# Two-layer attention and expert kernel on one Trainium2 core: stage loads moved, first preload in three portions, expert results scattered per token

## The reference

```python
x = L0_attn_X                                  # (2, 2048, 256): 4096 tokens of width 256
h = _layernorm(x) * (1 + ca) + sa              # sa, ca, ga, ... from _silu(L0_c) @ L0_wmod
x = x + ga * _L0_attn_ref(h, W_q, W_k, W_v, W_o)      # 16 heads of 16, RoPE, causal
h = _layernorm(x) * (1 + cb) + sb
x = x + gb * _L0_ffn_ref(h, gate_w, expert_w)         # 8 experts, one per token (argmax)
h = _layernorm(x) * (1 + ca) + sa              # the second layer's modulation from here
x = x + ga * _L1_attn_ref(h, ...)                     # gated mix along blocks of the sequence
h = _layernorm(x) * (1 + cb) + sb
x = x + gb * _L1_ffn_ref(h, ...)                      # RMS norm, softmax over the best 2 of 8
                                                      # experts, each silu(x W1a + b) * (x W1b + b) W2 + b2
```

## Time and profile before

| what | value |
|---|---|
| runs shown | 2666.26, 2665.64, 2662.68 us; median 2665.64 |
| profiled execution, its own time | 2663.03 us |
| its span | 2661.1 us, 39725 instructions |
| granted TensorE clock, mean | 0.916 of full speed |
| busy: PE, PE weight load | 2231.8 us (84%), 1413.0 us (53%) |
| busy: DVE, ACT, POOL | 1693.0 (64%), 1260.2 (47%), 859.6 (32%) |
| HBM read, written | 150.88 MB, 85.07 MB |
| stage ends (approximate) | modulation 47, projections 244, attention 1206, output projection 1268, first experts 1506, layer1 1827, routed experts 2559, combine 2661 |

### The profile page before, as it was taken

One profiled execution on the slowest core, in us unless ns is written; L12 is line 12 of the kernel. 1 busy time (PEld: TensorE's weight loads), 2 busy tenths in 40 slices (PEclk: granted clock), 3 DMA queues, 4 the chain that ended last, 5 costly groups with the idle time before them and its releaser, 6 DMA issues. The chain is left out here.

```text
span 2661.1 us, 39725 instructions
## 1 busy us (share of the span) xinstructions
PE 2231.8 (84%) x12968; PEld 1413.0 (53%) x12968; DVE 1693.0 (64%) x2599; ACT 1260.2 (47%) x2419; POOL 859.6 (32%) x1041
## 2 busy tenths in 40 slices
PE   3984898999989899996799699853999999999930
PEld 1762233333333333325577456553888888888830
DVE  4873877777777778844688768753545555545544
ACT  1331376766757677773223344412445555545520
POOL 2445302122121211110655413543223333323256
PEclk8996699999999999998899899966999999999975
DMA  4368604042140400002860100115444344434324
GB/s 164 107 144 166 91 2 65 5 62 35 33 65 3 64 3 3 2 1 67 351 256 0 31 1 17 40 44 182 136 152 141 133 149 141 146 121 133 123 76 126
DMA packets 138336, 238.26 MB, mean 90 GB/s; under 512 B 14768, under 2 KB 101552, under 8 KB 136752
## 3 DMA queue, kind: packets, MB, share of 16 engines
q1 hardware_dynamic: 122128, 181.44, 19.8%
q0 software_dynamic: 14928, 50.35, 10.7%
q10 hardware_dynamic: 1104, 4.20, 1.1%
HBM read 150.88 MB, written 85.07 MB: 89 GB/s over the span
## 5 line engine op out<-in xcount | busy, mean ns | idle before, releaser
L892 DVE TENSOR_REDUCE tile_max<-p_m 128x2 f32<-128x1024 f32 (+3 forms) x640 | 651.9, 1061 | 172.5 <-PE p_m L751 102.8
L854 ACT ACTIVATE probs<-p_s 128x512 f32<-128x512 f32 (+3 forms) x1280 | 596.3, 534 | 273.2 <-PE p_s L764 267.7
L2052 PE MATMUL p_up<-f_xT,f_w 128*128 128x512 f32 (+1 forms) x2304 | 468.9, 352 | 8.6 <-POOL f_w L2182 8.6
L2052 PEld LDWEIGHTS p_up<-f_xT,f_w 128*128 128x128 f32 x2304 | 372.2, 189 | 62.0 <-issue 8.9
L2182 POOL TENSOR_TENSOR f_w<-f_raw,f_w 128x1024 fp32r<-128x1024 f32 x96 | 230.9, 2409 | 504.0 <-ACT f_w L2104 504.0
L751 PE MATMUL p_m<-ka,qa 96*128 96x512 bf16 (+3 forms) x1280 | 363.3, 366 | 27.1 <-PEq L327 15.3
L705 POOL TENSOR_SCALAR_AFFINE_SELECT probs<-probs 128x128 f32<-128x128 f32 x512 | 143.3, 292 | 732.2 <-ACT probs L854 724.7
L764 PE MATMUL p_s<-qa,ka 99*128 99x512 bf16 (+3 forms) x1280 | 353.5, 353 | 11.5 <-ACT probs L854 6.9
L778 PE MATMUL p_o<-probs,va 128*32 128x512 f32 (+3 forms) x2560 | 305.9, 550 | 29.5 <-POOL probs L705 29.5
L2067 PE MATMUL p_y<-f_w,f_hidden 128*128 128x256 f32 x1872 | 261.8, 286 | 23.0 <-DVE f_y L2158 11.7
L2067 PEld LDWEIGHTS p_y<-f_w,f_hidden 128*128 128x128 f32 x1872 | 241.1, 188 | 45.4 <-issue 23.5
(11 more groups left out here) (242 smaller groups left out, 2602.3 us busy)
## 6 DMA issues: line engine op xcount, KB each, us to landing
y_slots<-zeros SPq DMA_DIRECT2D x73, 512.0 KB, 5.6
f_raw<-in_W1a SPq DMA_DIRECT2D x24, 1024.0 KB, 6.5
f_raw<-in_W1b SPq DMA_DIRECT2D x24, 1024.0 KB, 8.6
f_raw<-in_W SPq DMA_DIRECT2D x24, 1024.0 KB, 11.1
qk_scr<-parts SPq DMA_DIRECT2D x48, 256.0 KB, 2.3
qa<-qk_scr POOLq DMA_DIRECT2D x42, 256.0 KB, 15.6
ka<-qk_scr POOLq DMA_DIRECT2D x42, 256.0 KB, 17.4
v_scr<-wqkv_raw SPq DMA_DIRECT2D x32, 256.0 KB, 3.1
```

Of the source, the lines that this page charges most:

```text
L854: nc.scalar.activation(probs[:, (buf * UNITS + n) % NPROBS, h, lo:CH], p_s[:, s_bank(("exp", HG * n + h), buf), lo:CH], ACT.Exp, scale=DH ...
L892: nc.vector.tensor_reduce(out=tile_max[:, 2 * hp:2 * hp + 2, i, bank], in_=p_m[:, at_bank, :, 0:width], op=ALU.max, axis=AX.X).then_inc(ma ...
L2052: last = nc.tensor.matmul(p_up[:, f % 2, ab, 0:size], w1[:, wh, ab * KT + kt, f * P:(f + 1) * P], xT[:, t % 2, xh, kt, 0:size], start=(kt, ...
```

## The change

Eight edits; line numbers of the changed kernel are some ten to forty higher.

1. Projections: ACT's loop is written out, and the first stage's load is cut in three portions of 4, 4 and 5 DMAs, issued at the end of ACT's chunks 4, 5 and 6.
2. The ones rows of the first `ka` buffer are set by POOL in the projections, between its rstd and its subtracts of the weights; those of the other two after unit 11 of attention stage 0. At the start of stages 1 to 7 PE waits for them.
3. Attention: POOL issues the load of stage s + 2 after the masks of unit 11 (the last of the second chunk) of stage s, for s = 1 to 5, in place of stage s + 3 after stage s. Buffer and order of the loads are the same.
4. `top1_experts`: the zero fill and its memset are gone.
5. `layer1`: the rows of x are 258 wide; the two new columns are the token's number plus 1 and its first choice plus 1. DVE copies the numbers out of the route table before it centers, and waits for that table; each `choose` gets one more small operation, and `owner_ids` one.
6. `routed_experts`: DVE works out each row's place among the tokens (`find_rows`, five small operations, each waiting for the one before) behind `rest_of_x`, into three buffers `y_to`. POOL scatters a tile's result with them (4 or 2 indirect DMAs, L2216 of the changed kernel) into `y_rows`, where the first choices lie in token order and then the second ones; empty rows go to a dump row. SP's stores of y are gone; its load of x waits for `find_rows` of the tile before; `take_y` and, from t = 3 on, `find_rows` wait for scatters of earlier tiles.
7. `combine`: 16 plain loads of 512 KB by SP in place of the 64 gathers, ACT does the first weighting, DVE the rest, with all 8 chunks in SBUF at once.
8. Several semaphores are kept across stages and no longer cleared between them.

```diff
 def load_first_stage(third):          # ACT, projections
+    if third == 0:
         for qk in range(2):
             act.wait_ge(parts_stored[qk], 16 * SPLIT * CPS)
         act.wait_ge(va_stored, 16 * NHG * CPS)
-    load_scores_rows(act, k, 0, k.qa0, k.ka0, k.stage0_loaded)
-    load_values(act, k, 0, k.va0[:, :, :], k.stage0_loaded)
+    load_scores_rows(act, k, 0, k.qa0, k.ka0, k.stage0_loaded, range(2 * third, 2 * third + 2))
+    if third == 2:
+        load_values(act, k, 0, k.va0[:, :, :], k.stage0_loaded)
 def chunk(i, par):
-    if isinstance(i, int) and i == NCH - 2:
-        load_first_stage()
...
     split(i, 1)
+    if isinstance(i, int) and CPS <= i < CPS + 3:
+        load_first_stage(i - CPS)
...
 root(nc, pool, k, 0)                  # POOL, projections
+pool.wait_ge(k.rstd_ready, 1)
+nc.gpsimd.memset(k.ka0[QROWS:QROWS + SPLIT, :, :], 1.0).then_inc(ones0_set, 1)
+pool.wait_ge(ones0_set, 1)
...
 for s in range(1, NBUF):              # POOL, attention
     load(s)
-for rows in ka:
-    last = nc.gpsimd.memset(rows[QROWS:QROWS + SPLIT, :, :], 1.0)
-last.then_inc(ones_set, 1)
 for s in range(NS):
     for n in diag_no:
         mask(s, n)
-    if s + NBUF < NS:
-        load(s + NBUF)
+        if diag_no[n] == 2 * TPC - 1:
+            if s == 0:
+                pool.wait_ge(diag_masked, 2 * TPC)
+                for n1 in range(1, NBUF):
+                    nc.gpsimd.memset(ka[n1][QROWS:QROWS + SPLIT, :, :], 1.0).then_inc(ones_set, 1)
+                pool.wait_ge(ones_set, NBUF - 1)
+            elif s + NBUF - 1 < NS:
+                load(s + NBUF - 1)
...
-    with sp.Fori(0, NSLOT // ST) as t:          # SP, top1_experts
-        sp.dma_start(k.y_slots[at(t, ST, ST), :].rearrange("(p u) d -> p (u d)", p=P), zeros[:, :]
-                     ).then_inc(slots_zeroed, 16)
...
+dve.wait_ge(route_loaded, 16 * ROUTE_LOADS)     # DVE, layer1, ahead of center_h
+c_own.add(nc.vector.tensor_copy(row_ids[:, :, 0], token_no))
...
 if t:                                 # SP, routed_experts, load(t)
     sp.wait_ge(turned, t)
+    sp.wait_ge(y_to_ready, t)
...
+def find_rows(t):                     # DVE, routed_experts
+    blocks = SIZES[t] // P
+    dve.wait_ge(x_loaded, 16 * t + 16)
...
+    dve.wait_ge(second_ready, 4 * t + 4)
+    if t >= 3:
+        dve.wait_ge(y_stored, 16 * blocks_to[t - 2])
+    nc.vector.tensor_copy(y_to[:, t % 3, 0:blocks], second[:, 0:blocks]).then_inc(y_to_ready, 1)
...
     if t:                             # take_y(t)
-        dve.wait_ge(y_stored, 16 * t)
+        dve.wait_ge(y_stored, 16 * blocks_to[t])
...
 if f == TURN_AT and not last_tile(t):
     rest_of_x(t + 1)
+    find_rows(t + 1)
...
+def scatter(t):                       # POOL, after the four pieces of tile t + 1
+    pool.wait_ge(y_to_ready, t + 1)
+    pool.wait_ge(y_ready, t + 1)
+    for u in range(SIZES[t] // P):
+        pool.indirect_dma_start(out=k.y_rows[:, :],
+                                out_offset=bass.IndirectOffsetOnAxis(ap=y_to[:, t % 3, u:u + 1], axis=0),
+                                in_=y[:, u, :], in_offset=None).then_inc(y_stored, 16)
...
+for i in range(NCH):                  # SP, combine; all loads ahead of the stores
+    for q in range(2):
+        row = q * SECOND + 1 + i * CH
+        sp.dma_start(ys[:, q, rows_of(i), :], k.y_rows[row:row + CH, :].rearrange("(u p) d -> p u d", p=P)
+                     ).then_inc(loaded[i], 16)
...
+nc.scalar.activation(res[:, t, :], ys[:, 0, t, :], ACT.Copy, scale=k.weights[:, 0, t:t + 1])   # x32, ACT
+nc.vector.scalar_tensor_tensor(out=res[:, t, :], in0=ys[:, 1, t, :], scalar=k.weights[:, 1, t:t + 1],
+                               in1=res[:, t, :], op0=ALU.mult, op1=ALU.add)                  # x32, DVE
```

More of the change, by code:

```diff
@@ L135, in modulation @@
         product, copied, own = m.sem("mod_product"), m.sem("mod_copied"), m.sem("mod_own")
-        x_loaded = [m.sem(f"x_loaded{b}") for b in range(B)]
+        x_loaded = k.x_loaded
         LOADS = 6
@@ L270, in normalize, with load_scores_rows @@
     nc.vector.tensor_tensor(h, h, shift, ALU.add).then_inc(done, 1)
-def load_scores_rows(engine, k, s, qa, ka, loaded):
-    for g, (qp, kp) in enumerate(zip(Q_PARTS, K_PARTS)):
+def load_scores_rows(engine, k, s, qa, ka, loaded, groups=range(len(Q_PARTS))):
+    for g in groups:
+        qp, kp = Q_PARTS[g], K_PARTS[g]
         for dst, qk, part in ((qa, 0, qp), (ka, 1, kp)):
@@ L557, in attention @@
         p_o = m.ps("p_o", [P, CH])
-        stage_loaded = [m.sem(f"stage_loaded{n}") for n in range(NBUF)]
+        stage_loaded = k.stage_loaded
         scores_ready, probs_ready, probs_used = m.sem("scores_ready"), m.sem("probs_ready"), m.sem("probs_used")
@@ L802, in stage @@
                             pe.wait_ge(max_placed, 16 * (CPS * s + c + 1))
+                            if c == 0 and not first(s):
+                                pe.wait_ge(ones_set, NBUF - 1)
                         for pair in range(2):
@@ L1962, in routed_experts @@
         hidden_high, hidden_ready = m.sem("f_hidden_high"), m.sem("f_hidden_ready")
-        y_ready, y_stored = m.sem("f_y_ready"), m.sem("f_y_stored")
+        y_ready, y_stored = m.sem("f_y_ready"), k.y_stored
+        second_ready, y_to_ready, dump_set = m.sem("f_second_ready"), m.sem("f_y_to_ready"), m.sem("f_dump_set")
+        blocks_to = [sum(SIZES[:t]) // P for t in range(NTILES + 1)]
         pieces = [(1, 0), (2, 0), (1, 1), (1, 2), (2, 1), (1, 3)]
@@ L2162, in _ @@
                 rest_of_w2(0, 1)
+                for u in range(SPT):
+                    last = nc.vector.memset(dump_no[:, u:u + 1], float(-u))
+                last.then_inc(dump_set, 1)
+                dve.wait_ge(dump_set, 1)
+                find_rows(0)
                 for t in range(NTILES):
@@ L2189, in combine @@
         m = Mem(nc, stack)
-        ys = m.sb("g_ys", [P, 2, 2, TPC, D])
-        res = m.sb("g_res", [P, 2, TPC, D])
-        gathered = [m.sem(f"g_gathered{n}") for n in range(2)]
-        stored = [m.sem(f"g_stored{n}") for n in range(2)]
-        done, own = m.sem("g_done"), m.sem("g_own")
-        OWN = 2 * TPC + 1
+        ys = m.sb("g_ys", [P, 2, NT, D])
+        res = m.sb("g_res", [P, NT, D])
+        loaded, stored = [m.sem(f"g_loaded{i}") for i in range(NCH)], m.sem("g_stored")
+        weighed, summed, gated, done = (m.sem("g_" + n) for n in ("weighed", "summed", "gated", "done"))
```

144 lines of the change are left out of this document (71 added, 73 removed).

## The result

The changed kernel takes 2574.8 us (median of 4 runs, 2572.26 to 2577.1), the kernel before 2665.2 (4 runs); the ratio is 0.9662, with a 95% interval of 0.9645 to 0.9679. The forecast was 2575.6. The total is right; the parts are less so, and the rest of this document is about them.

The account below looks back on a forecast made before the run. PE was taken to bound attention and the routed experts, POOL's gather issue `combine`. Terms -34 - 15 + 6 + 7 - 54 = -90 took 2665.64 us to 2575.6; range 2562 to 2589, all bounds 2548 to 2615.

Parts of the forecast that it names:

- Attention -34: Attention: moving the loads gains 41 us gross over five stages and gives back 7; net -34, bounds -41 and -28.
- PE stands 0 to 2.4 us, and five times 1.4 gives back 7: Attention: PE waits for chunk 3's `place` in each of five stages holding a load, 1.4 us each, 7 in all.
- Does not come back until the load is drained: Attention: a store SP issues into a load returns only when that load is drained; 9.4 us in the kernel before.
- small transfers slip through: Rival: stores in attention and projections wait for no drain, giving -41 and -19; 11 us less, 2565; chance 0.15.
- Memsets 0, bound +5: Ones memsets moved from attention's start: two hidden in POOL's gap, the third before the projections' weight subtracts; 0, bound +5.
- Projections -15: Projections: 18.6 us of ACT's waits lost before; the split load's first two portions cost 0 to 1.5 each, the third up to 4.
- layer1 +6: `layer1`: waiting for the route table holds DVE's list, +5; six more small operations, +1; bounds 0 and +8.
- Routed experts +7: Routed experts: five chained DVE operations add 1 us in each of eight 256-row tiles; +7, bounds 0 and +12.
- so the 1 us lands on PE: Routed experts, 256-row tiles: DVE has no pause before the `hidden` PE's down product needs, so `find_rows` delays PE 1 us.
- costlier scatters and a costlier row search: Rival: scatters by fresh numbers, `take_y` waiting, `find_rows` at 2 us instead of 1; +15, 2591; chance 0.15.
- drawn-out scatters: Rival: each routed scatter takes 6.56 us beside DVE's work, as one in `layer1` did; +150, 2726; chance 0.04.
- End and combine -54: Routed stage's end +2, then `combine` with plain loads at 4.2 us a chunk, ending at 2607 against 2661.1; bounds -58, -40.

Follow-up runs that it names:

- the later load: Changed kernel with POOL's load of stage s + 2 issued after the masks of unit 23 (end of the third chunk) instead of unit 11: 2559.71 us.

## Why the prediction was right, point by point

The total was right within 1 us, and that is partly luck: by the table above the terms were off by some 50 us in sum of their sizes and by 3 net. Two of the signs that I had named for a wrong forecast came: stage distances of 109.6 to 114.8 us instead of 109.5, and 0.3 us instead of 1 in the 256-row tiles.

- *Attention -34*: measured -23.4 in the stages, in two parts. The gross gain is 584.3 - 547.2 = 37.0 us (the five stages before, and with the later load), where I had 41: the stage where the loop turns won only 5.1. The give-back is 13.6, where the step "PE stands 0 to 2.4 us, and five times 1.4 gives back 7" had 7. It was mis-sized, since three of the five pauses also lowered the granted clock; I had the same effect in the gain (8.2 us a stage for a stall of 6.0 us), and did not carry it over to the loss. That the store is held some 8 us and PE then waits 1 to 2 us was as forecast, and is shown by the later load. "Does not come back until the load is drained" was wrong as a rule (6.2 to 6.8 us for a store at the load's start), and gave the right time only because this store falls near its end. The rival that small transfers slip through is refuted: 8.0 us in the load, 1.4 outside.
- *Memsets 0, bound +5*: two steps were wrong. "The third stands ahead of the subtracts ... counted 0": +5.3, and +6.4 with the line below it in the table, outside the bound; not because the subtracts drew out, but because DVE's centering stood behind the memset. And "leave the start of attention, where PE works on maxima that don't need them": -5.5, as an operation of DVE stood behind the third of them. Together nearly 0. The two in the gap hid, as said.
- *Projections -15*: measured -17.4. The first two portions hide, the third costs 2.6.
- *layer1 +6*: +5.6 for the wait, shown by moving it. The small operations can't be told from the stage's variation.
- *Routed experts +7*: measured -5.6. That is +3.5 for the work and -9.1 from the shifted layout, which I had not thought of at all. The step "so the 1 us lands on PE" was mis-sized: about 0.3 us a tile did. I also misread the pattern of tiles: it is 15 tiles of 512 rows and 9 of 256, with 78 scatters (not 80), and a 256-row tile takes 23.3 us (not 18.3). "Eight such tiles" is right all the same, as the last one has no `find_rows`. The rivals of costlier scatters and a costlier row search fall for the change as it was. That of drawn-out scatters does too: the 78 of them took 0.95 to 0.99 us each.
- *End and combine -54*: measured -46.7. `combine` was right within 0.5 us; "the last scatter is two issues and a landing instead: +2" was wrong: +9.8, of which 8 are open.

## What to carry to other kernels

When a bulk load is moved off the path, look for the small store and read-back that will now be issued into it, and place the load behind the last of them that somebody waits for soon: that was worth 13.6 us of 37 here. Price a pause of PE at more than its length where its clock is at the upper level (8.3 us of pauses cost 13.6). "Hidden" needs the rows of the other engines too: a POOL memset that nobody waited for held a DVE operation of 0.2 us for 5.7 in one place, and DVE's centering for 7.1 in another. And slack can't be priced by making a chain longer: the second 0.9 us cost 1.7 a tile, the first 1 us had cost 0.3.

## What the runs showed of the hardware

- A change of addresses in SBUF alone made the same matmuls 13 us shorter in 690 (703.2 us for the stage instead of 712.3, one run each); another, of 32 bytes per partition, gave 715.0 and 715.1. So a change that adds a tile to a stage moves this too, and a difference of 1% in a stage bound by PE needs the layout as a control.
- Pauses of PE of 1.6 to 2.1 us in attention were followed by 6 to 12 us in which the granted clock averaged 0.70 to 0.73; after two of 1.3 us it stayed at 1.00. Longer pauses in eight tiles of the routed experts (7.4 us more in all) came with a clock of 0.98 in the whole stage instead of 1.00.
- A 12 KB store from SP's queue came back in 1.4 us with no load in flight. It came back in 6.7 to 11.4 us when issued 21 to 24 us into a load of 4.2 MB by POOL (before, changed kernel and later load), and in 6.2 to 6.8 when issued 1.2 us into one, long before that was drained.
- A DVE operation of 0.20 us stood 5.7 and 5.9 us while POOL wrote a memset of 6.9 us, in two kernels, and its row calls that busy; one of the centering stood 7.1 us behind another such memset. Reductions of DVE beside the same memsets did not stand.
